# Two-phase linear-attention block: passage between the phases reordered, attention stores moved to GpSimd's queue

## The reference, cut to what matters

```python
x = x + attn(layernorm(x), Wq, Wk, Wv, Wo, Wa, ba)      # x: (4, 2048, 512), 16 heads of 64
x = x + ffn(layernorm(x), CB, SCB, bias)

def attn(x, ...):                                       # gated linear attention
    q, k, v = x @ Wq, x @ Wk, x @ Wv ; q, k = elu(q) + 1, elu(k) + 1
    a = sigmoid(x @ Wa + ba + 2)
    S = a * S + k v^T ; z = a * z + k                   # a scan over the 2048 rows
    return ((q S) / (q z + 1e-6)) @ Wo
def ffn(x, ...):
    return (x @ CB.T) * (SCB / 127) + bias
```

## Time and profile before

| | us |
|---|---|
| median of 3 runs | 1980.44 |
| lowest and highest run | 1977.69, 1982.33 |
| the profiled execution: its time | 1982.77 |
| the profiled execution: its span | 1981.0 |
| TensorE busy in the span | 1943.0 (98%) |
| VectorE busy | 1652.1 (83%) |
| ScalarE busy | 691.2 (35%) |
| GpSimd busy | 389.6 (20%) |

### The profile page before, as it was taken

How to read it: one execution, slowest core, us unless ns; L and a number is a source line. 1 busy time by engine, 2 the same in 40 slices (tenths; PEclk the granted TensorE clock), 3 DMA queues, 4 the chain that set the end, 5 groups by cost and what they waited for, 6 DMA issues and landing times.

```text
span 1981.0 us, 69665 instructions
## 1 busy us (share of the span) xinstructions
PE 1943.0 (98%) x26926; PEld 1693.1 (85%) x26926; DVE 1652.1 (83%) x2918; ACT 691.2 (35%) x1288; POOL 389.6 (20%) x368
## 2 busy tenths in 40 slices
PE   7999999999999999999999999999979999999998
PEld 6888888888889888888888898888758888888886
DVE  7788888888888888888888888888867777777776
ACT  5333343334333433343334333433412222222221
POOL 3222222232222223322222232222010000000000
PEclk9999999999999999999999999999989999999999
DMA  7333343444344444443344444335457777777775
GB/s 214 88 92 97 98 116 95 109 106 109 94 99 99 110 100 107 106 104 96 97 107 102 109 105 107 96 96 133 107 143 192 193 195 194 191 193 193 194 192 142
DMA packets 604995, 253.66 MB, mean 128 GB/s; under 512 B 433056, under 2 KB 547232, under 8 KB 604960
## 3 DMA queue, kind: packets, MB, share of 16 engines
q1 hardware_dynamic: 569824, 221.20, 44.5%
q10 hardware_dynamic: 35136, 32.00, 5.8%
HBM read 184.84 MB, written 68.22 MB: 128 GB/s over the span
## 4 chain that ended last, share of the span: by engine, by line
PE 93%; DVE 2%; DMA 2%; SPq 1%; issue 1%; POOL 1%; ACT 0%; DVEq 0%; POOLq 0%
PE G L1330 53%; PE DS L1288 16%; PE NUM L1288 8%; PE NUM L1399 4%; PE SC L1452 3%; PE DS L1431 3%; PE NUM L1413 3%; PE SC L1278 2%; PE DS L1472 1%; DVE w_lo L922 0%; DMA out_rows<-xt 0%; DMA x_cols<-D 0%; DMA qT<-in_CBT 0%; SPq L431 0%; DMA norm_rows<-moments 0%
## 5 line engine op out<-in xcount | busy, mean ns | idle before, releaser
L1330 PE MATMUL G<-w_hi,xT_hi 128*128 128x512 f32 x1024 | 407.1, 398 | 1.3 <-DVE w_lo L922 1.3
L1330 PE MATMUL G<-w_lo,xT_hi 128*128 128x512 f32 x1024 | 399.9, 391 | 0.0
L1330 PE MATMUL G<-w_hi,xT_lo 128*128 128x512 f32 x1024 | 398.8, 389 | 0.0
L743 ACT ACTIVATE relu_t<-G 128x512 f32<-128x512 f32 x256 | 153.4, 599 | 454.0 <-PE G L1330 450.6
L1330 PE MATMUL G<-xT_hi,w_hi 128*128 128x256 f32 x1024 | 290.2, 283 | 0.2 <-DVE w_lo L922 0.2
L1330 PE MATMUL G<-xT_lo,w_hi 128*128 128x256 f32 x1024 | 289.8, 283 | 0.0
L1330 PE MATMUL G<-xT_hi,w_lo 128*128 128x256 f32 x1024 | 289.7, 283 | 0.0
L1330 PEld LDWEIGHTS G<-w_hi,xT_hi 128*128 128x128 f32 x1024 | 192.4, 188 | 43.1 <-DVE xT_lo L915 1.4
L1330 PEld LDWEIGHTS G<-w_hi,xT_lo 128*128 128x128 f32 x1024 | 192.3, 188 | 41.6
L1330 PEld LDWEIGHTS G<-w_lo,xT_hi 128*128 128x128 f32 x1024 | 192.6, 188 | 35.6
L1288 PE MATMUL DS<-w_hi 128*128 128x512 f32 x512 | 200.5, 392 | 0.5 <-issue 0.5
(11 more groups left out here) (137 smaller groups left out, 3610.8 us busy)
## 6 DMA issues: line engine op xcount, KB each, us to landing
abc<-decay_rows SPq DMA_DIRECT2D x256, 128.0 KB, 3.2
pbc<-product_rows SPq DMA_DIRECT2D x256, 128.0 KB, 3.1
attn_cols<-attn SPq DMA_DIRECT2D x512, 64.0 KB, 2.2
at_rows<-attn_cols ACTq DMA_DIRECT2D x244, 128.0 KB, 3.2
xt<-in_x SPq DMA_DIRECT2D x64, 256.0 KB, 3.0
x_in<-in_x SPq DMA_DIRECT2D x64, 256.0 KB, 2.9
out_rows<-xt SPq DMA_DIRECT2D x64, 256.0 KB, 3.0
xT_in<-in_xT SPq DMA_DIRECT2D x31, 512.0 KB, 4.5
```

What stands on the lines that cost most here:

```text
L743: act.activation(relu_t[buffer][:, :], bank[:, :], ACT.Relu)
L1330: made = nc.tensor.matmul(to, lhs, rhs, start=(n == 0), stop=(n == len(passes) - 1))
```

## The change

The stores of phase one move from SyncE's program to GpSimd's, behind its normalising in the same step. SyncE calls `ffn_weights()` in step NC right after `load_attn(2, 0)`. On GpSimd the inverse deviation of chunk 0 comes in step NC + 1 ahead of the last store, and the scaling of the weights behind that store. On VectorE the residual of chunk 0 comes ahead of the scale vector and of the last `normalised(1)`. ScalarE loads chunk 3 ahead of `ffn_weights_hi()`, and its wait for all stores moves to the load of chunk NC - 2. VectorE subtracts the turned x1 ahead of the transpose of chunk 1 and of `rows_lo` of chunk 3.

```diff
--- before.py
+++ after.py
@@ -421,17 +421,6 @@
                 sp.dma_start(bias_b[:, :], bias.rearrange("(a n) -> a n", a=1).broadcast_to([128, DM]))\
                     .then_inc(bias_loaded, 16)
 
-            def store_rows(r, n, count):
-
-                here = chunk_at(n)
-                sp.wait_ge(attn_ready[r], count)
-                for c in range(2):
-                    for half in range(2):
-                        q = 64 * c + SQ * half
-                        sp.dma_start(cols_of(here)[c, r, :, :, SQ * half:SQ * half + SQ],
-                                     attn[q:q + SQ, U * r:U * r + U].rearrange("f (b t) -> f b t", t=SQ))\
-                            .then_inc(attn_stored[r], 16)
-
             def load_x(n, b):
 
                 sp.dma_start(x_in[b][:, :], x_rows[bass.ds(row(sp, n), C), :]).then_inc(xin_loaded, 16)
@@ -539,8 +528,7 @@
                     for h in range(2):
                         sp.wait_ge(oT_lo_ready[h], 1)
                     load_attn(sp, 2, 0)
-                if exists(i - 2):
-                    store_rows(1, i - 2, one[-2])
+                    ffn_weights()
                 if b == 1 and exists(i):
                     products(1, this)
                 if gates:
@@ -560,10 +548,6 @@
                     sp.wait_ge(rows_loaded, 64)
                     sp.wait_ge(xin_loaded, 16)
                     load(1, 1)
-                if exists(i - 1):
-                    store_rows(0, i - 1, one[-1])
-                if isinstance(i, int) and i == NC:
-                    ffn_weights()
                 if isinstance(i, int) and i == NC - 4:
                     output_weights(0)
                 if isinstance(i, int) and i == NC - 2:
@@ -641,7 +625,22 @@
                 pool.wait_ge(vareps2_ready, count)
                 pool.tensor_tensor(rstd2[:, :], vareps2[:, :], minus_half[:, 0:1], ALU.pow).then_inc(rstd2_ready, 1)
 
+            def store_rows(r, n, count):
+
+                here = n
+                if not isinstance(n, int):
+                    here = pool.snap(n)
+                    pool.compute_val(here)
+                pool.wait_ge(attn_ready[r], count)
+                for c in range(2):
+                    for half in range(2):
+                        q = 64 * c + SQ * half
+                        pool.dma_start(cols_of(here)[c, r, :, :, SQ * half:SQ * half + SQ],
+                                       attn[q:q + SQ, U * r:U * r + U].rearrange("f (b t) -> f b t", t=SQ))\
+                            .then_inc(attn_stored[r], 16)
+
             def step(i, pair, b):
+                one = counts(pool, i, 1, (-2, -1))
                 if b == 0 and exists(i + 2):
                     pairs = counts(pool, pair, 1, (0, 1))
                     p16 = counts(pool, pair, 16, (0,))
@@ -656,12 +655,17 @@
                     for kt in range(KT):
                         made = pool.tensor_tensor(x4[:, kt, :, :], x4[:, kt, :, :], norm_b[:, 1, :, :], ALU.mult)
                     made.then_inc(xT_normal, 1)
-                if isinstance(i, int) and i == NC:
+                if isinstance(i, int) and i == NC + 1:
+                    inverse_deviation2(1)
+                if exists(i - 2):
+                    store_rows(1, i - 2, one[-2])
+                if exists(i - 1):
+                    store_rows(0, i - 1, one[-1])
+                if isinstance(i, int) and i == NC + 1:
                     pool.wait_ge(wf_loaded, 16 * KT)
                     pool.wait_ge(scaled, 1)
                     for kt in range(KT):
                         pool.tensor_tensor(raw_wf[kt], raw_wf[kt], scale, ALU.mult).then_inc(wf_scaled, 1)
-                    inverse_deviation2(1)
 
             def step2(i, _, b):
                 if exists(i):
@@ -861,8 +865,6 @@
 
                 if exists(i + 1):
                     rows_hi(r64[1], one[-1], 1 - b)
-                if isinstance(i, int) and i == 1:
-                    ffn_weights_hi()
                 if isinstance(i, int) and i == 2:
                     turned_hi(1, 0)
                 elif exists(i - 2):
@@ -875,12 +877,14 @@
                     if not isinstance(i, int):
                         ahead = act.snap(ahead)
                         act.compute_val(ahead)
-                    if isinstance(i, int) and i == 1:
+                    if isinstance(i, int) and i == NC - 4:
                         for r in range(2):
                             act.wait_ge(attn_stored[r], 64 * NC)
                     for r in range(2):
                         act.wait_ge(oT_lo_ready[r], one[0])
                     load_attn(act, ahead, b)
+                if isinstance(i, int) and i == 1:
+                    ffn_weights_hi()
                 if isinstance(i, int) and i == NC:
                     act.wait_ge(F_ready, NC - 2)
                     turned_hi(2, 1 - b)
@@ -1199,11 +1203,11 @@
                     if exists(i - r) and exists(i + 1 - r):
                         carried_on(r)
                 if isinstance(i, int) and i == NC + 1:
-                    normalised(1)
+                    residual(1, 16, 0)
+                    residual_deviation(1)
                     dve.wait_ge(scale_loaded, 16)
                     nc.vector.tensor_scalar(scale, scale, 1.0 / 127.0, None, ALU.mult).then_inc(scaled, 1)
-                    residual(1, 16, 0)
-                    residual_deviation(1)
+                    normalised(1)
 
             steps(dve, step, -1, NC + 2)
 
@@ -1220,6 +1224,8 @@
 
                 if exists(i - 1):
                     residual_normal(one[-1], 1 - b)
+                if isinstance(i, int) and i == 2:
+                    turned_lo(1, 0)
                 if exists(i - 2) and exists(i):
                     dve.wait_ge(x1n_ready, one[-1])
                     if exists(i - 4):
@@ -1228,9 +1234,7 @@
                                         x1n[1 - b].rearrange("p (b f x) -> p x b f", f=SQ, x=4)).then_inc(x1t_ready, 1)
                 if exists(i + 1):
                     rows_lo(one[1], 1 - b)
-                if isinstance(i, int) and i == 2:
-                    turned_lo(1, 0)
-                elif exists(i - 2) and exists(i - 1):
+                if exists(i - 3) and exists(i - 1):
                     dve.wait_ge(fT_hi_ready, one[-2])
                     nc.vector.tensor_tensor(fT_lo[b], fT_in[b], fT_hi[b].bitcast(fp32), ALU.subtract)\
                         .then_inc(fT_lo_ready, 1)
```

## The result

The changed kernel takes 1989.95 us (median of four, 1985.09 to 1992.64) beside 1980.1 for the kernel before (1977.69 to 1982.33): ratio 1.0047, 95% interval 1.0029 to 1.0065. It is slower by half a per cent; the forecast was 1976.1 by its sum, faster. The profiled execution is the quickest of the four, 1985.09 us, span 1983.4.

What follows compares the result with a forecast made beforehand. TensorE was taken as the bound, busy 1943.0 of 1981.0 us. A passage gain of 4.3 us (6.95 less 2.65), phase one at 0, took 1982.77 to 1978.5, or 1976.1 in the median's terms; range 1967 to 1990.

Steps and rivals of the forecast that it cites:

- Part 1: SyncE: weight loads issued earlier, at 1435.7 instead of 1442.58; losing its stores in phase one is worth 0 there.
- the stores stand behind the normalising ... covered, 0: Phase one: a store is up to 11 us later, its buffer overwritten only a 22 us step later; cost 0.
- a pair of steps over 43.8 us: Phase one: one of the signs named beforehand that would show the forecast wrong.
- a chance of 0.22: Whole kernel: chance given to slower, beside 0.50 for faster and 0.28 for no change.
- x, the price of a store on GpSimd: GpSimd's queue: time per store, taken as 1.1 us, between 0.63 from below and 3.0 from above.
- GpSimd becomes the bound: Rival, GpSimd's queue in phase one: slower if x passes about 1.6, 2130 to 2230 us at x = 2; chance 0.17.
- stores are cheap: Case with x of 0.75 and no fall of the clock: gain 11.2 us, 1969 us; chance 0.15.
- GpSimd's stores stretch VectorE: Rival, phase one: stores slow VectorE, a few tenths to 1 us a pair, 1985 to 2010 us; chance 0.05.
- the first hole: Passage: TensorE's idle wait for VectorE's normalised x1 shrinks from 12.0 to 2.7 us, no fall of the clock charged.
- second hole: Passage: TensorE idle 5.2 us before the first feed-forward product at 1458.7, with 2.65 us of half speed charged.
- The gain of the passage, 4.3 us: Passage: first feed-forward product 6.95 us earlier, less 2.65 us for half speed.
- second fall of the clock: Passage, at the 5.2 us hole before the first feed-forward product: clock drops to half speed again, costing 2.65 us.

Runs made afterwards that it cites:

- e2: Kernel before with only the 512 stores moved to GpSimd, the passage left as before: 1991.92 us, ratio 1.0077.
- e3: Changed kernel with one more wait on GpSimd: in odd steps the store of half 0 waits until the product loads have landed; 1972.76 us, ratio 0.9979.
- e6: Kernel of e3 with GpSimd's inverse deviation and four weight scalings put ahead of the stores of chunk 63: 1969.67 us, ratio 0.9967.

## Why the prediction was wrong

- **Part 1, phase one on SyncE ("worth 0 there"), and "the stores stand behind the normalising ... covered, 0".** This is the step that failed. I asked whether TensorE waits for anything in phase one before (it doesn't) and whether a store may be *later*. It isn't only later: in the odd steps, where GpSimd normalises nothing, it goes out 3.4 us *earlier* (+3.87 against +7.25), ahead of the product loads it used to follow. SyncE's queue had been an order of urgency; two queues have none. 500.00 of 500.00 told that there was no loss, not how far off one was: the slack was some 1.2 us of `pc`. Put at 0, the term measures 13.3 us in the loop (14.8 by the medians of e2); in e3 one wait takes it away. I named "a pair of steps over 43.8 us" among the signs of an error, but none of my rivals had this mechanism. The right sign came with a chance of 0.22 for other reasons. That 1989.95 lies just inside the range is luck: its upper end of 1990 was set by GpSimd as the bound or VectorE stretched, and neither happened.
- **x, the price of a store on GpSimd: 1.1 us forecast, 0.65 measured.**

```profile
L638 POOL DMA_DIRECT2D attn_cols<-attn x512: 620/647/874, 64.2 to 1459.4; - x171
```

It is near the lower bound, SyncE's 0.63: starting from an arithmetic instruction's 0.55 us and adding a part for GpSimd's slowness on elements made it too high. So "GpSimd becomes the bound" falls (16 x 0.65 = 10.4 us of stores in a pair), and for x the case "stores are cheap" was the true one. With x at the measured value the sum has no loss in phase one, so the price was not what made the forecast wrong.
- **GpSimd's stores stretch VectorE:** no. VectorE's 770 instructions in 500 us take 0.562 us each against 0.557. Its arithmetic does: the addition of the bias (L991) took 5.10 us beside the scaling in e3 and 0.69 beside stores in e6; in the changed kernel (L988, shown above) it took 1.56 beside the scaling, so how long varies.

```profile
1446.04 5.10 DVE L991 TENSOR_TENSOR exp_t<-relu_t,bias_b 128x512 f32<-128x512 f32 x1
```

```profile
1447.43 0.69 DVE L991 TENSOR_TENSOR exp_t<-relu_t,bias_b 128x512 f32<-128x512 f32 x1
```

The Trainium skill (SBUF — State Buffer, Who interferes with whom) has two-input VectorE operations held up by GpSimd's reads; here the trace agrees, and the operation outlasted several of GpSimd's (5.10 against some 1.3 each). I had priced this at nothing on the way to the first feed-forward product.
- **The passage:** the first hole was forecast at 2.7 and is 2.75, by luck, from two errors that cancel: the eight stores ahead of the inverse deviation are 3.6 us cheaper (8 x 0.45), and one stall of 3.50 us stands among them that no row of before could show. The clock did fall again:

```profile
1457.50:1458.00 0.50, 0.00 (x0) 0.00 (x0) 0.50 (x2) 0.00 (x0) 0.50 (x1) 0.79 0.14 33
1458.00:1458.50 0.50, 0.41 (x8) 0.44 (x8) 0.50 (x2) 0.00 (x0) 0.50 (x2) 0.50 0.03 10
...
1464.50:1465.00 0.50, 0.50 (x3) 0.39 (x3) 0.50 (x2) 0.50 (x1) 0.50 (x1) 0.88 0.00 0
```

It fell at about 1457.8, when TensorE had stood idle since 1455.35, and was at 1.2 GHz until about 1464.6. "The fall before came only after more idling than that, so I charge none" was wrong. I had charged a fall, but to the second hole; it belongs to the first.
- **The second hole** (5.2 us forecast) is 1.08 us in the changed kernel. Output product 2 starts 2.2 us behind the transposes instead of 1.15, since VectorE's subtraction ahead of it takes 2.35 us for two beside the scaling, and then takes 7.7 us instead of 5.4, much of it at half speed; the rest is that the scaling ended earlier against the hole than forecast.
- **The gain of the passage, 4.3 us,** was 6.95 us for an earlier start of the feed-forward part less 2.65 for the second fall of the clock. The first term held: against the end of the work ahead of the hole the start comes 7.65 us earlier in the changed kernel and 7.2 in e3. The second doesn't show: the fall lies ahead of that start, inside the 7.65, and what follows the start takes 514.3 and 514.1 us beside 515.4. The medians of e3 do give 4.3 us (1972.76 against 1977.1), but this doesn't confirm the sum: it had the second term wrong, and single executions of one kernel differ by 4 us.

## What to carry to other kernels

A queue that gives out several streams of DMAs also puts them in order. Before a stream is moved to another engine's queue, write down for each of its DMAs when it will go out now and which urgent load it will be ahead of, in every step of the loop and not only where it comes later; an engine that is never idle in the trace says nothing of how near the next wait is. If the order matters, restore it with one wait on the urgent load's semaphore: here that turned 1.0047 into 0.9979.

## What the runs showed of the hardware that was not expected

- DMAs from one queue delay those from another though the DMA engines' mean share is 0.39 to 0.44: four stores of 64 KB, given out 1.1 us ahead of the product loads, bring the start of `pc` behind them from +8.8 to +10.8. The Trainium skill (DMA: Bandwidth & Descriptors, Issuing engines are not separate DMA queues) says that all engines' DMAs run on the same 16 DMA engines and that issuing from several of them only saves issue time. The trace agrees with the first, in that the early stores make the loads land late from whichever of two queues they come (57.6 us of waiting from GpSimd's, 47.7 with ScalarE's, 22.3 behind the loads); of the second it shows the other side, that the order of one queue is lost.
- A store of 512 runs of 128 bytes holds GpSimd 0.647 us at the median, SyncE 0.628 and ScalarE 0.600. Four in a row in the loop take 2.58, 3.02 and 2.9 us. From issue to landing a store takes 2.6 us from GpSimd (2.2 to 5.6), 2.2 from SyncE (2.1 to 4.8) and 3.3 from ScalarE (2.2 to 5.1).
- The same 512 stores count as far fewer packets from GpSimd. The queues of the kernel before and of the changed one (packets, MB, share of the 16 engines; `q0` holds GpSimd's 33.59 MB):

```profile
q1 hardware_dynamic: 569824, 221.20, 44.5%
```

```profile
q1 hardware_dynamic: 299488, 187.61, 34.0%
q0 software_dynamic: 16384, 33.59, 9.4%
```

  That is 32 packets a store from GpSimd against 528 from SyncE, and 9.4% of the engines' time against 10.5%: by this count too GpSimd's stores are not the heavier ones.
- GpSimd's idle time before some of its stores, 0.3 to 1.1 us ahead of the passage and 3.5 in it. Eight DMAs more at the start don't shift it to other stores; its cause is open (total, times, longest):

```profile
POOL attn_cols L638 <- issue: 13.9, 14, 3.5
```

- Beside GpSimd's scaling, VectorE's operations with two inputs can take far more than their own time: 5.10 us in e3 and 1.56 in the changed kernel for 0.69, and 3.42 in e6 for 1.28. So in these kernels scaling the weights on GpSimd is not free for VectorE even where GpSimd has the time.
